# The build of a graph network's count matrix: loops over halves and chunks of five engines written out

## The reference

```python
edge_index = jnp.stack([src, dst])
h = jnp.maximum(_layernorm(x), 0.0); x = x + _L0_gnn_ref(h, src, dst)          # degree-normed sum over neighbours
h = jnp.maximum(_layernorm(x), 0.0); x = x + _L1_gnn_ref(h, edge_index, ...)   # two attention layers
h = jnp.maximum(_layernorm(x), 0.0); x = x + _L2_gnn_ref(h, edge_index, ...)   # one attention layer, row norm
h = jnp.maximum(_layernorm(x), 0.0); x = x + _L3_gnn_ref(h, edge_index, edge_weight1, ...)  # two message layers, log softmax
return x
```

## Time and profile before

| What | Value |
|---|---|
| Median of 3 runs | 2841.45 us |
| The profiled execution | 2841.15 us, span 2838.9 us |
| Mean granted TensorE clock | 0.942 |
| Busy: PE, DVE, ACT, POOL | 86%, 78%, 55%, 15% |
| The build: first to last window matmul | 230.4 to 950 us |
| Wait of PE for DVE's first keys, ahead of 230.4 us | 19.7 us |

### The profile page before, as it was taken

The page is one execution under the profiler, slowest core; times in us unless marked ns, Lnnn a source line. Parts: engine busy times, 40 slices in busy tenths (PEclk is TensorE's granted clock), DMA queues, the critical chain, the costliest instruction groups (busy, mean ns, idle before and its releaser), DMA issues. The chain is left out here.

```text
span 2838.9 us, 86445 instructions
## 1 busy us (share of the span) xinstructions
PE 2431.0 (86%) x31023; PEld 2188.3 (77%) x31024; DVE 2203.5 (78%) x4979; ACT 1548.5 (55%) x1943; POOL 424.0 (15%) x921
## 2 busy tenths in 40 slices
PE   2656999999999679999599998769999868999998
PEld 2644777677777569988599888669999858898997
DVE  8986899898899879999799899799999984222212
ACT  6004444444444289998799987588888740000101
POOL 1003555555556300000000000000000000000000
PEclk8877999999999889999899999989999979999999
DMA  3003443533435347676356655225655437888998
GB/s 107 0 0 87 127 127 88 166 87 108 145 87 149 99 160 266 234 265 215 104 189 205 226 181 181 91 92 183 204 181 181 158 115 247 308 306 299 330 366 299
DMA packets 398046, 494.28 MB, mean 174 GB/s; under 512 B 81925, under 2 KB 397289, under 8 KB 397674
## 3 DMA queue, kind: packets, MB, share of 16 engines
q1 hardware_dynamic: 364760, 487.44, 51.0%
q10 hardware_dynamic: 33044, 3.63, 1.0%
HBM read 401.81 MB, written 89.17 MB: 173 GB/s over the span
## 5 line engine op out<-in xcount | busy, mean ns | idle before, releaser
L2740 PE MATMUL psum<-sb_arena 128*128 128x99 bf16 (+2 forms) x13524 | 1011.3, 236 | 127.7 <-DVE sb_arena L2010 82.6
L2740 PEld LDWEIGHTS psum<-sb_arena 128*128 128x128 f16 x13524 | 969.7, 99 | 157.2 <-DVE sb_arena L2010 103.0
L3366 ACT ACTIVATE sb_arena<-sb_arena 128x896 f16 (+1 forms) x980 | 961.7, 1036 | 152.4 <-PE psum L2740 107.4
L2000 DVE TENSOR_TENSOR sb_arena<-sb_arena 128x896 f16<-128x896 f16 x980 | 593.0, 621 | 84.9 <-ACT sb_arena L3366 55.2
L3035 ACT ACTIVATE sb_arena<-psum 128x784 f16<-128x784 f32 x392 | 322.5, 823 | 394.6 <-PE psum L2385 226.5
L1280 DVE TENSOR_SCALAR sb_arena<-sb_arena 128x392 f16<-128x392 f16 x1960 | 486.9, 323 | 0.0
L2385 PE MATMUL psum<-sb_arena 64*128 64x392 f16 x3920 | 387.0, 341 | 70.1 <-ACT sb_arena L3035 25.0
L2835 PE MATMUL psum<-sb_arena 128*128 128x192 bf16 x4802 | 416.2, 248 | 30.4 <-DVEq L2157 15.2
L2835 PEld LDWEIGHTS psum<-sb_arena 128*128 128x128 f16 x4802 | 402.5, 98 | 46.0 <-DVEq L2157 16.1
L2010 DVE TENSOR_TENSOR sb_arena<-sb_arena 128x896 f16<-128x896 f16 x686 | 424.0, 618 | 0.3
L2385 PEld LDWEIGHTS psum<-sb_arena 64*128 64x128 bf16 x3920 | 258.3, 138 | 151.3 <-issue 79.8
(11 more groups left out here) (381 smaller groups left out, 1444.5 us busy)
## 6 DMA issues: line engine op xcount, KB each, us to landing
sb_arena<-counts SPq DMA_DIRECT2D x245, 896.0 KB, 6.9
sb_arena<-counts SPq DMA_DIRECT2D x245, 672.0 KB, 4.6
counts<-sb_arena SPq DMA_DIRECT2D x56, 1344.0 KB, 6.7
sb_arena<-records SPq DMA_DIRECT2D x392, 5.0 KB, 2.1
sb_arena<-records ACTq DMA_DIRECT2D x392, 5.0 KB, 2.2
counts<-sb_arena SPq DMA_DIRECT2D x1, 5488.0 KB, 19.8
records<-sb_arena SPq DMA_DIRECT2D x1, 3124.0 KB, 8.9
counts<-sb_arena SPq DMA_DIRECT2D x14, 112.0 KB, 4.6
```

What stands on the lines that cost most here:

```text
L2000: nc.vector.tensor_tensor(above_at[r % RING], above_at[r % RING], counts_of(g, j), ALU.mult).then_inc(above_ready, 1)
L2740: last = nc.tensor.matmul(psum[:, bank, at:at + wide], of[:, b * BLK:(b + 1) * BLK], moves[side][:, r, 0:wide], start=(r == 0 and at == 0) ...
L3366: nc.scalar.activation(above_at[r % RING], of, ACT.Sigmoid, bias=steep_s[:, r:r + 1], scale=STEEP).then_inc(signs_ready, 1)
```

## The change

The five engines' loops over halves and chunks of the build become Python loops, so each pass is written out with its own numbers. ACT's seven chunks are one loop, POOL's six are written out ahead of the seventh. Conditions that asked whether h was a register ask for its number. The store's slices are plain slices of the same place. What is computed, the order of each engine's operations, the buffers and the semaphores are as before.

```diff
-                with sp.Fori(0, NH) as h:
+                for h in range(NH):
                     for k in range(WH):
                         sp.wait_ge(rel_ready, h * WH + (k + 1))
-                        packed = sp.value_load(starts[0:1, bass.ds(h * 2 * WH + group_of(k, 0), 1)], min_val=0, ...)
+                        packed = sp.value_load(starts[0:1, h * 2 * WH + group_of(k, 0):h * 2 * WH + group_of(k, 0) + 1], min_val=0, ...)
...
-                            sp.dma_start(counts[:, a0:a1, bass.ds(h, 1), :].rearrange("b a o d -> b a (o d)"),
-                                         ap1(stage[:, bass.ds((h + 1) % 2, 1), a0 * HALF:a1 * HALF]).rearrange("p (a d) -> p a d", d=HALF)).then_inc(counts_stored, 16)
+                            sp.dma_start(counts[:, a0:a1, h, :],
+                                         stage[:, (h + 1) % 2, a0 * HALF:a1 * HALF].rearrange("p (a d) -> p a d", d=HALF)).then_inc(counts_stored, 16)
...
-                with pool.Fori(0, CHUNKS - 1) as c:
+                for c in range(CHUNKS - 1):
                     for odd in range(2):
                         half_of_build(c, odd, WH + AHEAD)
...
-                with dve.Fori(0, NH) as h:
+                for h in range(NH):
                     for k in range(WH):
...
-                        if i == i1 - 1 and p % 2 == 1 and not isinstance(h, int):
+                        if i == i1 - 1 and p % 2 == 1 and h < NH:
                             pe.wait_ge(ea_ready, h * (WH // EG) + (p // 2 + 2))
...
-                with pe.Fori(0, CHUNKS) as c:
+                for c in range(CHUNKS):
                     for odd in range(2):
...
-                    if not isinstance(h, int) or h <= NH:
+                    if h <= NH:
                         act.wait_ge(ea_used, h * (WH // EG) + (HITS - 1))
...
-                with act.Fori(0, CHUNKS - 1) as c:
+                for c in range(CHUNKS):
                     chunk_of_build(c)
-                chunk_of_build(CHUNKS - 1)
```

More of the change, by code:

```diff
@@ L726, in _ @@
             with sp.If(fast == 1):
-                with sp.Fori(0, NH) as h:
+                for h in range(NH):
                     for k in range(WH):
                         sp.wait_ge(rel_ready, h * WH + (k + 1))
-                        packed = sp.value_load(starts[0:1, bass.ds(h * 2 * WH + group_of(k, 0), 1)], min_val=0, max_val=(TILES * BLK - CAP) * PACK)
+                        packed = sp.value_load(starts[0:1, h * 2 * WH + group_of(k, 0):h * 2 * WH + group_of(k, 0) + 1], min_val=0, max_val=(TILES * BLK - CAP) * PACK)
                         sp.dma_start(rec[0:SIDE, k % RS, :], records[bass.ds(packed // PACK, CAP), :].rearrange("(p t) c -> p (t c)", p=SIDE)).then_inc(rec_in[k % RS // 2], 16)
```

## The result

The changed kernel takes 2792.65 us in the median (four runs, 2790.56 to 2797.1); the kernel before took 2841.33 beside it. The ratio is 0.983, with a 95% interval of 0.9818 to 0.9842. So the change is worth 1.7%; the forecast was 2781 us, 11.7 us less, and the range (2767 to 2803) holds the result.

What follows compares the result with a forecast made beforehand. TensorE (PE), the busiest engine at 86%, was taken to need 46.27 us a half; gains of 21.7 + 11.75 + 26.4 = 59.84 us from 2841.15 gave 2781 us (-2.1%), range 2767 to 2803.

Steps and rivals of the forecast that it cites:

- The signs named for the forecast: Build: no PE issue wait at L2385, clock 1.00 from second half, thirteen halves of 46.3 us, build some 662 us.
- The start: First half of the build, 14.18 us over the pace; prologue code is unchanged, so all of it stays.
- PE's branch and the slow clock: Six PE stops before later passes, 21.7 us, and the slow clock after them, 11.75 us; both go.
- the lost cover of ACT's branch: At each pass turn PE's stop covers ACT's branch; both go in the same diff, so nothing is lost.
- The slow stretch: Halves 2 to 12: PE waits as ACT's address reads slow during SP's stores; ACT's and POOL's constants gain 26.4 us.
- rival A: Slow stretch stays: at full pace ACT at 1.87 us a window meets the stores every half; 2807.7 us, chance 0.14.
- the next one, on SP: SP in the build: loads issue as early or earlier, stores keep their queue places; its constants are worth 0 by themselves.
- Register instructions of PE: PE's 378 ALU_OPs at L2380 are hidden behind matmuls: gain 0, bounds no gain and 12.1 us.
- DVE and POOL: Their register instructions in the build run beside longer work, DVE having 5 us to spare a half: worth 0.
- Rival C: Slower: DVE's straight code in the build needs some 22 instruction fetches that may stop it; up to 2864 us, chance 0.04.
- Stages behind the build: The stages after the build were to take as long as before.

Runs made afterwards that it cites:

- e4: Kernel before with only ACT's build loop written out; PE, SP, DVE and POOL keep their loops: 2816.78 us, ratio 0.9906.
- e2: Kernel before with SP, DVE, POOL and ACT written out, PE keeping its loop: 2821.53 us, ratio 0.9922.
- e1: Kernel before with only PE's loop written out; SP, DVE, POOL and ACT keep theirs: 2833.60 us, ratio 0.9973.
- e3: Kernel before with PE's and ACT's loops written out; SP, DVE and POOL keep theirs: 2806.19 us, ratio 0.9873.
- e5: Kernel before with PE's, ACT's and SP's loops written out; POOL and DVE keep theirs: 2791.38 us, ratio 0.9822.
- e9: Changed kernel, but SP also waits for PE's window 4 of the half before its first store of the counts: 2782.70 us, ratio 0.9793.
- e6: Changed kernel with DVE's loop left as it was, all other engines written out: 2790.11 us, ratio 0.9818.

## Why the prediction was right, and where it missed

The signs named for the forecast came in part: no stop is left, the clock is 1.00 and ACT's distance during the stores is still 1.87 us, but halves 2 to 14 take 46.97 us in the mean and not 46.3, and the build 670.8 us and not 662.

*The start, kept at 14.18 us:* right for this change (60.18 against 60.45 us).

*PE's branch and the slow clock, 21.7 + 11.75 us:* right as a pair. No stop is left, and the clock is 1.00 from the second half on. e4 shows both by themselves at 34.4 us; taken away last they are worth 28.9, since the changed kernel loses some 4 us more at the seams than e2 (9.5 us over the pace, where e2 has 5.9 beside the stops and the slow clock). The figure of the Trainium skill (Advanced Engine Details and Errata, section Control Flow Timing), 108 ns, doesn't describe what PE's branch costs here: 3669 ns in e2's row, and its gain would have been 21 us smaller. The sentence that the lost cover of ACT's branch doesn't matter "as it sits in the same diff" was needed: in e1, without that part, the stop came back under ACT's name.

*The slow stretch, 26.4 us:* this is the term that was mis-sized, at 26.4 - 9.1 = 17.3 us. "ACT's and POOL's constants are enough" is true with SP in its loop and PE's stops in place, as e4 shows (POOL's aren't even needed), and it was read from a last pass in which both were so: the first store of half 13 went out while PE still stood at its branch, 2.1 us ahead of PE's first matmul, and in half 14 ACT stops loading. That this pass lost nothing was in part luck, as rival A had warned. But the step that failed is the next one, on SP: that its stores stay "in the same places of its queue" and its constants are "worth 0 by themselves". Two runs contradict it, from both sides. Without SP's constants the rest of the change loses some 24 us from the seventh half on (e3 against e5), because 49.3 us a half is more than 46.2. With them SP arrives early, so that its first store goes out 1.05 to 1.2 us behind the seam and meets ACT's late moment (e9). The stores kept their place in the queue and lost their place in time. SP's need hid in the kernel before behind PE's stops and the slow stretch, which gave it time to catch up. The meeting doesn't depend on the stops: e2 has them and loses 5.9 us, in those halves in which the store comes behind the seam, while e3 has none and loses nothing in halves 2 to 6, where SP is still in its loop and the first store comes 4 to 17 us behind the seam.

*Register instructions of PE, 0:* right; the best halves take 46.17 us, as PE's busy time does.

*DVE and POOL, 0:* right in the sum (e5, e6), with a wrong reason. "DVE has 5 us to spare in a half" was read from the last half with its 147 operations; a half in the middle has 162 and 45.81 us of busy time out of 46.17.

*Rival A* (ACT at 1.87 us meets the stores at full pace) happened by a third, and the half of it lay in the range. Its mechanism was the right one, apart from the place of the store. *Rival C:* 18 of the fetches on q14 come with DVE's code (119 against 101 in e6), where 22 were estimated; the 27 more of the page are the sum over four engines, with ACT's code taking 15 fewer (92 in e1, 77 in e3) and SP's 17 more (94 in e5). DVE has no wait without a releaser in the build; the fetches cost nothing there, so the trace agrees with the Trainium skill (Runtime: NRT & Kernel Launch, section Instruction fetch mechanics), which calls the crossing of a block mostly hidden, and not with C. *Stages behind the build* were to take as long as before and took 3.5 us more in the one execution that was profiled, which is within the spread; the jump of DVE, 2.3 us longer, may be a part of it.

## What to carry to other kernels

A stop that several engines share hides what each of them lacks; before it is removed, add up for each engine, the DMA issuing one too, what it needs for a whole round, and compare that with the new pace. An engine that gets faster off the path moves the start of its transfers: look at what they meet there. And a wait of the profile is checked by when the engine it names had finished; where that was long before, look for another that ended just then.

## What the hardware showed beyond that

ACT's read of one address takes 281 ns in the median and 887 while the stores run. One read of four addresses takes 311 ns in the median and up to 979, but there are two or three slow ones in a half and not eight, so fewer, wider reads are the cheap remedy. The time that a branch costs is not that of its instruction: ACT's lasts 52 ns, and ACT's next instruction starts 2.6 us later (e1); the time behind the same DVE jump goes from 0.58 to 2.84 us when the code ahead of it is written out. PE's jump over the other case went the other way, 3593 ns before and 379 after; it is 3358 to 3778 in the four kernels with PE's loop and 379 in the nine without:

```profile
L2395 PEldq COMPARE_BRANCH  x1: 379/379/379, 920.8 to 920.8; - x1
```

What decides between the short and the long form was not tried.
